# Row maxima of the first attention: two banks used in turn for differences and bases, and both relus of a step in one place on ScalarE

## The reference, cut to what matters

```
x = _group_norm(input, gn_weight, gn_bias)
qkv = jnp.einsum('bchw,oc->bohw', x, qkv_weight)
...
attn = jnp.einsum('bnchw,bncyx->bnhwyx', q, k) / math.sqrt(C)
attn = jax.nn.softmax(attn.reshape(B, N_HEAD, H, W, H * W), axis=-1)
...
out = jnp.einsum('bnhwyx,bncyx->bnchw', attn, v).reshape(B, C, H, W)
```

## Time and profile before

| what | us |
|---|---|
| median of 3 runs | 363.89 |
| span of the profiled execution | 384.2 |
| TensorE busy in it | 334.2 |
| VectorE busy | 202.1 |
| ScalarE busy | 204.4 |
| values of step 1 to values of step 31 (starts) | 50.97 to 138.84 |

### The profile page before, as it was taken

The page is one execution under the profiler, slowest core; times in us unless marked ns, Lnnn a source line. Parts: engine busy times, 40 slices in busy tenths (PEclk is TensorE's granted clock), DMA queues, the critical chain, the costliest instruction groups (busy, mean ns, idle before and its releaser), DMA issues.

```text
span 384.2 us, 6582 instructions
## 1 busy us (share of the span) xinstructions
PE 334.2 (87%) x2004; PEld 211.5 (55%) x2004; DVE 202.1 (53%) x616; ACT 204.4 (53%) x324; POOL 110.8 (29%) x140
## 2 busy tenths in 40 slices
PE   7879799899999989999998496967551999999996
PEld 3533343333333335445432354867551999999996
DVE  2584444563756553565576248666402455777620
ACT  1460765666576554655585023665212677777732
POOL 2082291000000001000307630061774344444430
PEclk9985989999999999999999879996665899999999
DMA  6078768660000025000001102010211222222415
GB/s 186 2 149 194 170 146 333 154 243 34 0 2 3 3 72 149 0 2 1 2 0 43 55 8 62 16 28 23 62 62 34 64 72 70 71 66 79 143 37 210
DMA packets 21772, 29.28 MB, mean 76 GB/s; under 512 B 4055, under 2 KB 15628, under 8 KB 21484
## 3 DMA queue, kind: packets, MB, share of 16 engines
q1 hardware_dynamic: 16808, 18.04, 17.7%
q0 software_dynamic: 3744, 10.31, 8.4%
q10 hardware_dynamic: 1188, 0.53, 0.6%
HBM read 11.62 MB, written 9.25 MB: 54 GB/s over the span
## 4 chain that ended last, share of the span: by engine, by line
PE 70%; DVE 13%; issue 6%; another core or an unknown queue 4%; ACT 3%; DMA 1%; POOL 1%; DVEq 0%; SPq 0%; ACTq 0%; POOLq 0%
PE ps L864 15%; PE ps L1081 10%; PE ps L1068 9%; PE ps L845 6%; PE ps L826 6%; DVE above L1189 4%; PE ps L706 2%; PE ps L806 2%; PE ps L922 2%; PE ps L746 2%; PE ps L899 2%; PE ps L778 1%; PE ps L891 1%; DMA Qs<-mrow 1%
## 5 line engine op out<-in xcount | busy, mean ns | idle before, releaser
L558 ACT ACTIVATE probs<-ps 128x1024 f32<-128x1024 f32 x64 | 65.3, 1021 | 37.0 <-PE ps L845 36.9
L1081 PE MATMUL ps<-w,GT 128*128 x368 | 55.0, 297 | 18.8 <-ACT GT L684 15.0
L864 PE MATMUL ps<-probs,vT 128*32 128x512 f32 x256 | 68.2, 608 | 1.1 <-ACT probs L558 1.1
L864 PE MATMUL ps<-probs,ones 128*32 128x512 f32 x256 | 68.2, 609 | 0.0
L1081 PEld LDWEIGHTS ps<-w,GT 128*128 128x128 f32 x368 | 49.3, 208 | 22.0 <-issue 21.7
L1189 DVE CUSTOM_DVE_ANT_0 above<-ps,above 128x512 f32<-128x512 f32 x56 | 38.7, 691 | 40.8 <-PE ps L826 39.0
L496 POOL DMA_INDIRECT token_out<-Y,yidx x46 | 44.2, 961 | 48.2 <-DVE Y L1480 46.6
L433 POOL TENSOR_TENSOR rstd<-ve,minus_half 128x1 f32<-128x1 f32 (+2 forms) x6 | 10.3, 1724 | 160.6 <-DVE ve L1231 88.6
L1068 PE MATMUL ps<-XTT,w1s 128*128 128x128 f32 x368 | 53.1, 291 | 3.2 <-issue 3.2
L684 ACT ACTIVATE GT<-H 128x512 f32<-128x512 f32 x46 | 28.9, 629 | 46.5 <-DVE H L1469 27.4
L1068 PEld LDWEIGHTS ps<-XTT,w1s 128*128 128x128 f32 x368 | 49.2, 208 | 4.3 <-issue 4.3
(11 more groups left out here) (196 smaller groups left out, 427.5 us busy)
## 6 DMA issues: line engine op xcount, KB each, us to landing
expert_in<-zeros POOLq DMA_DIRECT2D x2, 1495.0 KB, 7.6
XR<-expert_in SPq DMA_DIRECT2D x46, 65.0 KB
Qs<-q_hi SPq DMA_DIRECT2D x16, 128.0 KB, 3.1
w<-in_L_ffn_W SPq DMA_DIRECT2D x1, 2048.0 KB, 8.4
w<-in_L_ffn_W SPq DMA_DIRECT2D x8, 256.0 KB, 4.1
YG<-token_out SPq DMA_DIRECT2D x8, 256.0 KB, 4.1
Ks<-k_hi SPq DMA_DIRECT2D x14, 128.0 KB, 2.6
X<-in_x SPq DMA_DIRECT2D x2, 512.0 KB, 4.6
```

The costliest lines, as they stand in the source:

```text
L558: nc.scalar.activation(probs[:, s % 3, :], bank(2 + 2 * (s % 2), 2), ACT.Exp).then_inc(exp_done, 1)
L864: last = nc.tensor.matmul(bank(6 + o % 2)[i * HD:(i + 1) * HD, :], w, probs[:, s % 3, hd * HALF:(hd + 1) * HALF], start=kt == 0, stop=kt = ...
L1081: last = nc.tensor.matmul(bank(4 + p)[:, 0:D], GT[:, p, c, :], w2[:, e, c, :], start=c == 0, stop=c == HC - 1)
```

## The change

The two banks become a ring. Every use of a bank by a difference or a base has a place in a list `uses`, and successive uses take banks 1, 0, 1, 0. In a step with two ordinary slots the list reads difference g0, difference g1, base g0, base g1; so difference g0 and base g0 share bank 1, difference g1 and base g1 share bank 0. A use waits for whoever reads the use two places before it: a base for its own slot's relu (`above_ready`), a difference for the reduction of the slot two back (`slot_used`). A row slot has only the base's use. In a step with one ordinary and one row slot, or with one slot, the number of uses is odd or two, and the waits come out by the same rule.

The loops are rewritten to that order. TensorE: difference g0, scores of s + 1, difference g1, base g0, base g1, values of s. ScalarE: exponential of s, relu g0, relu g1. VectorE's order stays. The computation is the same.

```
-        def before_in(g, slots):
-            return max((x for x in slots if x < g and slot_banks(x) == slot_banks(g)), default=None)
+        RING_BANKS = (1, 0)
+        uses = [(g, half) for g in range(PLAIN_FIRST + 1, AHEAD) for half in (0, 1)]
+        for s in range(2 * STEPS):
+            new = new_slots(s)
+            uses += [(g, 0) for g in new[0:2]] + [(g, 1) for g in new[0:2]] + [(g, half) for g in new[2:] for half in (0, 1)]
+        uses = [(g, half) for g, half in uses if half or order[g][1] != "rows"]
+        nth_use = {use: n for n, use in enumerate(uses)}
+        def ring_bank(g, half):
+            return RING_BANKS[nth_use[g, half] % len(RING_BANKS)]
...
+        def use_before(g, half):
+            n = nth_use[g, half]
+            return uses[n - len(RING_BANKS)] if n >= len(RING_BANKS) else None
...
                 exps(s // STEPS, s % STEPS)
-                if s:
-                    for g in new_slots(s - 1)[1:]:
-                        max_above(g)
+                for g in new_slots(s):
+                    max_above(g)
                 run_parts(layer1, LAYER1_AT, s, 0)
-                for g in new_slots(s)[0:1]:
-                    max_above(g)
...
+            def wait_bank(g, half):
+                before = use_before(g, half)
+                if before is None:
+                    pe.wait_ge(slot_used, PLAIN_FIRST)
+                elif before[1]:
+                    pe.wait_ge(slot_used, before[0] + 1)
+                else:
+                    pe.wait_ge(above_ready, nth_folded[before[0]] + 1)
...
-                for g in new[0:1]:
-                    max_second(g)
                 for g in new[1:2]:
                     max_first(g)
+                for g in new[0:2]:
+                    max_second(g)
...
                 for hd in range(2):
                     values(s // STEPS, s % STEPS, hd)
-                for g in new[1:2]:
-                    max_second(g)
```

More of the change, by code:

```diff
@@ L267, in slot_banks, with base_bank @@
             return (6, 7) if g == PLAIN_FIRST else (0, 1)
-        def before_in(g, slots):
-            return max((x for x in slots if x < g and slot_banks(x) == slot_banks(g)), default=None)
+        RING_BANKS = (1, 0)
[7 more added lines that the diff above has]
+            return RING_BANKS[nth_use[g, half] % len(RING_BANKS)]
+        def base_bank(g):
+            return ring_bank(g, 1) if (g, 1) in nth_use else slot_banks(g)[0]
+        def use_before(g, half):
+            n = nth_use[g, half]
+            return uses[n - len(RING_BANKS)] if n >= len(RING_BANKS) else None
         BEGIN_LAYER1 = 2 * STEPS + 1
@@ L550, in max_above @@
                         act.wait_ge(slot_used, folded[n - 2] + 1)
-                    nc.scalar.activation(above[:, n % 2, :], bank(slot_banks(g)[1]), ACT.Relu).then_inc(above_ready, 1)
+                    nc.scalar.activation(above[:, n % 2, :], bank(ring_bank(g, 0)), ACT.Relu).then_inc(above_ready, 1)
             def exps(u, step):
@@ L794, in max_first @@
                         pe.wait_ge(stack_in[u], 16 * 12)
[L795 to L799, removed]
+                wait_bank(g, 0)
                 hd, t = i // QH, QH * qh + i % QH
@@ L802, in max_first @@
                 q = Qs[0:SPLIT, b, n, t * P:(t + 1) * P]
[L803 to L809, removed]
+                if g == folded[0] or u != order[folded[nth_folded[g] - 1]][0] // 2:
+                    pe.wait_ge(kd_in[u], 16 * 6)
+                nc.tensor.matmul(bank(ring_bank(g, 0)), q, Kd[0:SPLIT, b, n, :], start=True, stop=True).then_inc(diff_ready, 1)
             def max_second(g):
@@ L814, in max_second @@
                 b = u // PAIRS
[L815 to L818, removed]
+                if (g, 1) in nth_use:
+                    wait_bank(g, 1)
+                else:
+                    pe.wait_ge(slot_used, g - 1)
+                o = bank(base_bank(g))
                 if i == "rows":
@@ L1175, in max_slot @@
                 k, i = order[g]
-                base, other = slot_banks(g)
+                base = base_bank(g)
                 dve.wait_ge(slot_ready, g + 1)
```

## The result

The changed kernel takes **373.09 us** (median, 372.92 to 373.27, 4 runs); the kernel before, on the same chip, 363.56 (361.95 to 364.35, 4 runs). The ratio is **1.0269** (95%: 1.0245 to 1.0292). 371.8 was forecast, within 367 to 376.5.

A forecast was written before the change was run, and what follows sets the result against it. TensorE's queue was taken to set the pace in steps 4 to 31. +6.6 us over the 30 steps and +1.3 in the opening, +7.9 in all, were added to the median for 371.8 us, range 367 to 376.5.

The forecast's parts named there:

- The step of two slots: Attention steps with two ordinary slots: 3.33 us against 2.95, one VectorE wait of 0.24 gone, two ScalarE waits added.
- The other steps: Attention steps with row slots or one slot: 3.09 (4 steps), 2.41 (2), step 15 2.14, step 31 1.85 us.
- R1's wait: Scores of step 8 standing 1.12 us for R1's DMA: 0 to 0.3 stays, taken as 0.
- That slack also covers VectorE's softmax sums in steps 9, 17 and 25: Reductions done by 2.45 and 3.2, ahead of differences at 3.33 and 4.15, so these sums cost nothing.
- The opening: Steps 0 and 1, partly at low clock: relu g1 delays the values, +1.3 us, bounds 0.5 to 2.
- 22 x 3.33 + ...: Sum over 30 steps, values of step 1 to those of step 31: 94.4 us against 87.87, +6.6.
- Adding the sum to the median: Whole kernel: +7.9 us added to the median, not the 384.2 us span, giving 371.8; scaled it would be 7.5.
- the whole delay passes through: Behind step 31: nothing changes and every wait hangs on the attention's results, so the full delay reaches the end.
- The weight load of a waiting base: At base matmuls on TensorE: load begins only when the wait ends, values follow 0.43 behind instead of 0.33.
- The rival of hidden weight loads: At base g1: load already in place, values 0.33 behind, 2.2 us less, 369.6 us; chance 0.05.
- The relus in time: Rival at base g1: relu ends before TensorE arrives, pair step 2.62 us, about 356 us; chance 0.07.
- The clock falling in the attention: Rival in attention steps: stalls bring 1.2 GHz stretches, 1.2 us each, five more give 378 us; chance 0.07.

The follow-up runs named there:

- e1: Changed kernel with TensorE issuing base g1 behind the values again, ring and ScalarE's order kept: 362.18 us, ratio 0.9982 to the kernel before.
- e2: Changed kernel with both differences issued ahead of the next step's scores: 366.3 us, ratio 1.0103 to the kernel before.
- e3: Changed kernel with ScalarE's old order, relu g1 behind the next exponential: 397.08 us (one run).
- e5: Changed kernel with four matmuls on constants, results unused, added in TensorE's gaps in step 0: 370.08 us, ratio 1.0191 to the kernel before.
- before, again: Second profile of the kernel before, unchanged: 363.26 us (one run), span 361.5 us.
- e10: Kernel before with only the 3 MB DMA of zeros held until the small DMA that step 8's scores wait for has landed: 363.62 us, ratio 0.9997.
- e7: e1 with a third bank in the ring in steps where the other accumulator's bank is free: 359.97 us, ratio 0.9906 to the kernel before.
- e6: Kernel before with four matmuls on constants, results unused, added in the two gaps of step 0: 363.01 us, ratio 0.9996.
- e8: e7 with the 3 MB DMA of zeros held as in e10: 357.91 us, ratio 0.9871 to the kernel before.
- e4: Kernel before with only ScalarE's order changed, both relus of a step behind its exponential: 363.56 us, ratio 1.0003.
- e9: e8 with the four matmuls of e5 added in step 0: 356.99 us, ratio 0.9831 to the kernel before.

## Why the prediction was right

- **The step of two slots** was right: 3.33 forecast, 3.31 measured, with each start within 0.02 of the row that it was built from. The removed wait on VectorE was 0.24, the two new ones on ScalarE are 0.14 and 0.36 (forecast 0.13 and 0.38): difference g1 hands the array on at 112.69 + 0.24 and base g0 starts at 113.07, base g0 hands it on 0.34 later and base g1 starts at 113.77. e1, e2 and e3 show that the cause is the way difference g1, relu g1, base g1, values: with base g1 behind the values the step is 2.95, with difference g1 earlier 3.09, with relu g1 later 4.02.
- **The other steps**, as the prediction names them: 3.09 for a row slot and an ordinary one, as forecast; 2.39 in the reverse order (2.41); with step 15's one slot 2.13 (2.14); with step 31's row slot 1.77 (1.85). R1's wait is gone, step 6 is 3.31. From step 2 to step 31 the cost is 6.08 us, and 6.18 was forecast. Part of that agreement is luck: some 0.02 less in each step of two slots makes up for the 0.38 of the next point.
- **"That slack also covers VectorE's softmax sums in steps 9, 17 and 25"** failed in one step of three: step 17 took 3.69. Timeline of the changed kernel:

```profile
104.66 0.72 DVE L1220 STREAM_TRANSPOSE rec<-ps 64x512 f32<-64x512 f32 x1
...
105.42 0.69 DVE L1203 CUSTOM_DVE_ANT_0 above<-ps,above 128x512 f32<-128x512 f32 x1
...
106.17 0.19 PEld L824 LDWEIGHTS ps<-Kd,Qs 96*128 96x128 f32 x1 [0.53 <-DVE pm L1203]
```

  The sums stand ahead of the reduction there, and difference g1 waited for it. The term was left at nothing and is 0.38.
- **The opening** was mis-sized. Its mechanism was right, in that relu g1 delays the values of step 0 and the lengthened step falls into a low clock. Timeline of the changed kernel:

```profile
44.69 1.08 ACT L567 ACTIVATE above<-ps 128x512 f32<-128x512 f32 x2
...
45.82 0.28 PEld L842 LDWEIGHTS ps<-Ks,Qs 96*128 96x128 f32 x1 [0.30 <-ACT above L567]
...
46.53 1.06 PE L880 MATMUL ps<-probs,vT 128*32 128x512 f32 x1
```

  From the start of relu g0 to the values it is 1.84 us, where the earlier trace rows have 1.08: 0.76 more, not the 0.49 that was laid down, because base g1 itself already runs at the low clock and the values follow it by 0.71 instead of 0.43. The +0.53 of the table meets the forecast by chance, since the two executions come to relu g0 0.23 us apart (44.92 and 44.69). The step that failed is the sum over the 30 steps, "22 x 3.33 + ...", which counted step 1 at full clock, and the opening's term, which let the low clock end with step 0: it lasted some 10 us instead of 3.4, and step 1 took 5.06. That is 1.7 of the 2.0 us between the forecast sum of 7.9 and the 9.9 up to step 31; step 0 adds 0.4, within its bounds, and the later steps take 0.1 back. e5 confirms the size from the other side: without the low clock the changed kernel is some 3 us faster. What made the stretch longer stays open: ahead of it TensorE stood for 0.87 and 0.96 us (43.88 and 45.33), but before, again, shows 0.86 and 0.95 in the same places, and no run varied the stalls behind its start alone. The length varies between executions too: e10, which has the instructions of the kernel before up to there, had 6.8 us where both profiles of before have 3.4. The two traces with both bases ahead of the values and difference g1 behind the scores (the changed kernel and e3) are the only ones with some 10.
- **Adding the sum to the median** rather than to the long profiled execution was right, and "the whole delay passes through" as well: behind step 31 the two traces differ by 0.1. The median came out only 1.3 above the forecast, although the added time was 9.5 and not 7.9, because the kernel before stood at 363.56 beside it and not at 363.89.
- **The weight load of a waiting base** begins at its release, as the row said: base g1's starts at 113.77, 0.05 behind its relu's end, and the values follow it by 0.43 (113.77 to 114.20). The Trainium skill ("TensorE: Matmul & The Clock Gate", section "Architectural detail: the array is 16× 32×32, not 1× 128×128") says that TensorE's queue can pull weight loads ahead of matmuls in flight. For a load whose matmul has to wait, this trace shows no such thing. The rival of hidden weight loads did not come.
- **The relus in time** (about 356) did not come: relu g1 ends 1.03 behind the start of its difference (112.69 to 113.72), where 1.04 had been laid down. **The clock falling in the attention** did not come at 3.31 us, but e3 shows it at 4.02.

## What to carry to other kernels

Look at what stands between a result's producer and its next user in the queue, and lay that cover beside the length of the hand-over: here difference, relu and release take 1.08, a base took 0.34 of that, and the 0.99 of the values had been the cover. A rotation of buffers moves a wait to the next pair that shares one (e1: from base g0 to difference g1); it takes a buffer more to remove most of it (e7). And a gain in one place is only worth what the next DMA or the next low clock lets through: e6 shortens step 0 by 1.2 us, e10 takes a large DMA out of the way of a small one, and both leave the time as it is; with a ring of three the second of them takes 3.6 us off step 6 (e8).

## What the runs showed of the hardware that was not expected

The clock fell inside the attention, among steps that all looked alike. Steps of 3.31 us with 0.50 of stalls ran at 1.00 throughout; of the steps of 4.02, with 0.90 idle ahead of base g1, four had a stretch at the 1.2 GHz level and the others none (e3). In the opening the low stretch was 3.4 us long in both profiles of before and in e1, e2, e7 and e8, 6.8 in e4 and e10, some 10 in the changed kernel and e3, and there was none in e5, e6 and e9, the three with the added matmuls. Those four matmuls, which compute nothing, were worth some 3 us in the changed kernel and nothing in the kernel before; in the ring of three the medians are 0.9 apart (357.91 and 356.99), which their intervals do not tell from nothing.
